# Edge bias from ScalarE to TensorE, and gather indices read straight from kept tables, in a four-layer graph network

## What is computed

```
loop = arange(N); src = concat(src, loop); dst = concat(dst, loop)
deg = segment_sum(1, dst);  dinv = rsqrt(deg)
xw = h @ W0
agg = segment_sum(xw[src] * (dinv[src] * dinv[dst]), dst) + b0
x = x + where(agg >= 0, agg, a0 * agg)
```

## Time and profile before

| | before |
|---|---|
| median of 3 runs | 2609.81 us (2604.56 to 2611.62) |
| profiled execution | 2608.14 us, span 2606.6 us |
| mean granted TensorE clock | 0.912 |
| PE busy | 1899.9 us (73%) |
| DVE busy | 2027.9 us (78%) |
| ACT busy | 1725.7 us (66%) |
| POOL busy | 1311.4 us (50%) |
| DMA | 446.18 MB, mean 171 GB/s |

### The profile page before, as it was taken

The page is one execution under the profiler, slowest core; times in us unless marked ns, Lnnn a source line. Parts: engine busy times, 40 slices in busy tenths (PEclk is TensorE's granted clock), DMA queues, the critical chain, the costliest instruction groups (busy, mean ns, idle before and its releaser), DMA issues. The chain is left out here.

```text
span 2606.6 us, 48448 instructions
## 1 busy us (share of the span) xinstructions
PE 1899.9 (73%) x9715; PEld 1275.5 (49%) x9715; DVE 2027.9 (78%) x8016; ACT 1725.7 (66%) x4230; POOL 1311.4 (50%) x1309
## 2 busy tenths in 40 slices
PE   2445668888855666578884899566663999999996
PEld 1134445555534555468883444233332555555553
DVE  6855579999968999688885888588885777777773
ACT  3655679999965777589991444699994444444441
POOL 6755656666637666277760000000002677777773
PEclk9878889999986888889996999799997999999998
DMA  7989986666645777556662443699996544445540
GB/s 134 220 147 183 153 203 193 198 195 195 194 130 159 222 223 224 176 165 198 201 181 72 128 129 86 185 305 308 305 308 215 128 100 107 106 113 114 115 106 21
DMA packets 376244, 446.18 MB, mean 171 GB/s; under 512 B 103667, under 2 KB 225338, under 8 KB 376082
## 3 DMA queue, kind: packets, MB, share of 16 engines
q1 hardware_dynamic: 309970, 368.09, 50.8%
q0 software_dynamic: 59840, 74.08, 12.3%
q10 hardware_dynamic: 6272, 2.06, 0.5%
HBM read 288.86 MB, written 185.03 MB: 182 GB/s over the span
## 5 line engine op out<-in xcount | busy, mean ns | idle before, releaser
L2380 POOL DMA_INDIRECT mlp_bx<-t_X,k_bslot x2 | 2.0, 1012 | 611.7 <-POOLq L2647 611.4
L526 POOL DMA_INDIRECT second_xs<-t_XX,second_irs x200 | 205.4, 1027 | 115.8 <-issue 49.3
L2398 POOL DMA_INDIRECT out_dram<-mlp_ou,mlp_iro x200 | 212.6, 1063 | 83.2 <-issue 71.3
L2391 POOL DMA_INDIRECT mlp_xs<-t_X,mlp_irs x200 | 213.8, 1069 | 80.7 <-issue 55.7
L526 POOL DMA_INDIRECT project_xs<-t_XX,project_irs x200 | 199.6, 998 | 62.9 <-issue 58.3
L526 POOL DMA_INDIRECT a_xd<-in_x_dram,a_ird x152 | 152.6, 1004 | 129.1 <-DVE first_xo L968 84.9
L2439 DVE TENSOR_TENSOR_SCAN mlp_ms<-mlp_fm,mlp_ms,mlp_mm 128x500 f32<-128x500 f32 x98 | 123.4, 1260 | 120.2 <-ACT mlp_mm L2515 112.9
L2515 ACT ACTIVATE mlp_mm<-mlp_ps_m,mlp_bn 128x500 f32<-128x500 f32 x100 | 67.7, 677 | 187.1 <-PE mlp_ps_m L2575 187.1
L2265 PE MATMUL x_ps_o<-x_ht,x_wd 128*128 128x512 f32 (+1 forms) x198 | 117.1, 675 | 97.2 <-DVE x_ht L2165 81.1
L2575 PE MATMUL mlp_ps_m<-mlp_e,mlp_wn 128*128 128x504 f32 x400 | 185.3, 586 | 0.0
L2562 PE MATMUL mlp_ps_e<-mlp_h,mlp_we 128*128 128x504 f32 x400 | 179.5, 592 | 2.9 <-DVE mlp_h L2448 1.5
(11 more groups left out here) (411 smaller groups left out, 6343.3 us busy)
## 6 DMA issues: line engine op xcount, KB each, us to landing
first_x<-in_x_dram SPq DMA_DIRECT2D x97, 256.0 KB, 4.3
t_XX<-first_x SPq DMA_DIRECT2D x97, 256.0 KB, 2.7
project_x<-t_XX SPq DMA_DIRECT2D x97, 256.0 KB, 3.3
x_x<-t_XX SPq DMA_DIRECT2D x97, 256.0 KB, 4.3
t_X<-x_x SPq DMA_DIRECT2D x97, 256.0 KB, 3.7
out_dram<-x_ou SPq DMA_DIRECT2D x97, 256.0 KB, 4.7
t_XR<-in_x_dram SPq DMA_DIRECT2D x23, 1000.0 KB, 13.4
t_G<-second_g SPq DMA_DIRECT2D x50, 267.8 KB
```

What stands on the lines that cost most here:

```text
L526: pool.indirect_dma_start(dst[:, q, lo:hi], None, table, bass.IndirectOffsetOnAxis(ap=idx[:, q:q + 1], axis=0)).then_inc(s_rows, 16)
L2391: pool.indirect_dma_start(Xs[u][:, q, :], None, T["X3"], bass.IndirectOffsetOnAxis(ap=irs[u][:, q:q + 1], axis=0)).then_inc(s_rows[u], 16)
L2398: pool.indirect_dma_start(out, bass.IndirectOffsetOnAxis(ap=iro[s][:, q:q + 1], axis=0), OU[s][:, q, :], None, bounds_check=N - 1, oob_is_ ...
```

## The change

The edge bias: L1042 is left out. VectorE's blend L958 takes the product z straight from PSUM in place of the biased Re, so Re = Qe * (1 - a0) + z. TensorE first writes the bias into all four tiles of psE with one matmul (a row of ones, 1 x 126, against the row b01r, 1 x 512), and then, after the wait for VectorE, adds Re turned by four plain matmuls against the identity that accumulate, in place of four transposes. TensorE's later waits for psY are on e_p (VectorE has read it) in place of e_q (ScalarE has). b01r is loaded in prep by four small DMAs on SyncE's queue, ahead of b1c, and VectorE adds b1 to it.

The indices: the ring copies and their semaphores go, in the first, second, project and mlp phases. GpSimd gathers (and in mlp scatters) with columns of the kept tables, and its bodies are written out (`straight`) in place of looped (`steps`), as the columns must be constants.

```diff
@@ prep @@
+        for q in range(GT):
+            sp.dma_start(kp.b01r[:, q, :], a["L0_gnn_b"].partition_broadcast(1)).then_inc(s_w, 16)
-        dve.wait_ge(s_w, 16 * (8 + GT))
+        dve.wait_ge(s_w, 16 * (8 + 2 * GT))
+        dve.tensor_tensor(kp.b01r[:, :, :], kp.b01r[:, :, :], kp.b1[0:1, :, :], ALU.add)
-        pe.wait_ge(s_w, 16 * (8 + GT))
+        pe.wait_ge(s_w, 16 * (8 + 2 * GT))
@@ first, GpSimd @@
-            gate(kp, pool, e_idx, t + 1)
+            src, dst = kp.srci[:, t * GT:(t + 1) * GT], kp.dsti[:, t * GT:(t + 1) * GT]
...
-                gather_rows(pool, Xs[u], T["XR"], irs[u], s_rows[u], 0, XR)
+                gather_rows(pool, Xs[u], T["XR"], src, s_rows[u], 0, XR)
...
-        steps(pool, NGE, 10, 0, body)
+        straight(NGE, 0, body)
@@ first, VectorE @@
-        def indices(g, s):
-            if there(g, NGE) and not before(g, 4):
-                dve.wait_ge(s_rows[s], complete(g - 4, s) + gathered[s])
-                dve.tensor_copy(irs[s][:, :], kp.srci[:, bass.ds(g * GT, GT)])
-                dve.tensor_copy(ird[s][:, :], kp.dsti[:, bass.ds(g * GT, GT)]).then_inc(e_idx, 1)
...
-            indices(t + 3, (u + 3) % 4)
...
-                dve.scalar_tensor_tensor(Re[:, :, :], Qe[:, :, :], kp.oma[:, 0:1], Re[:, :, :], ALU.mult, ALU.add).then_inc(e_p, 1)
+                z = psY[:, 0:W4].rearrange("p (q e) -> p q e", q=GT)
+                dve.scalar_tensor_tensor(Re[:, :, :], Qe[:, :, :], kp.oma[:, 0:1], z, ALU.mult, ALU.add).then_inc(e_p, 1)
@@ first, ScalarE @@
-                act.activation(Re[:, :, :], z, ACT.Identity, bias=kp.b01[:, 0:1])
@@ first, TensorE @@
                 if h == 1 and not before(t, 1):
-                    pe.wait_ge(e_q, t)
+                    pe.wait_ge(e_p, t)
...
             if there(g2, NGE):
-                pe.wait_ge(e_p, g2 + 1)
                 if not before(g2, 1):
                     pe.wait_ge(e_x1, g2)
+                pe.matmul(psE[0:RW, :], kp.ones[0:1, 0:RW], kp.b01r[:, :, :].rearrange("p q d -> p (q d)"),
+                          start=True, stop=False, skip_group_check=True)
+                pe.wait_ge(e_p, g2 + 1)
                 for q in range(GT):
-                    ins = pe.transpose(psE[0:RW, q * 128:(q + 1) * 128], Re[:, q, :], kp.ident[:, :])
+                    ins = pe.matmul(psE[0:RW, q * 128:(q + 1) * 128], Re[:, q, :], kp.ident[:, :],
+                                    start=False, stop=True, skip_group_check=True)
                 ins.then_inc(e_b, 1)
...
                 if not before(g1, 1):
-                    pe.wait_ge(e_q, g1)
+                    pe.wait_ge(e_p, g1)
@@ second; project alike with kp.idx2 @@
-                gate(kp, pool, s_idx, t + 1)
...
-                gather_rows(pool, Xs[u], T["XX"][0:ROWS, :], irs[u], s_rows[u])
-
-        steps(pool, NGE, 1, 0, body)
+                gather_rows(pool, Xs[u], T["XX"][0:ROWS, :], kp.idx[:, t * GT:(t + 1) * GT], s_rows[u])
+
+        straight(NGE, 0, body)
@@ mlp @@
-                gate(kp, pool, s_idx, t + 1)
...
-                                            bass.IndirectOffsetOnAxis(ap=irs[u][:, q:q + 1], axis=0)).then_inc(s_rows[u], 16)
+                                            bass.IndirectOffsetOnAxis(ap=kp.idx[:, t * GT + q:t * GT + q + 1], axis=0)).then_inc(s_rows[u], 16)
...
-                gate(kp, pool, s_io, g + 1)
...
-        steps(pool, NGE, 8, 0, body)
+        straight(NGE, 8, body)
...
-                dve.tensor_copy(iro[s][:, :], kp.sidx[:, bass.ds(g * GT, GT)]).then_inc(s_io, 1)
```

More of the change, by code:

```diff
@@ L212, in __init__ @@
         self.b01 = sb("b01", [128, 1])
+        self.b01r = sb("b01r", [1, GT, 128])
         self.oma = sb("oma", [128, 1])
@@ L715, in phase_first @@
     nb = [sb(f"nb{i}", [128, 2 * XD]) for i in range(2)]
-    Xs, Xd, irs, ird = kp.Xs, kp.Xd, kp.irs, kp.ird
+    Xs, Xd = kp.Xs, kp.Xd
     Xo = [sb(f"xo{i}", [RW, GT, 128]) for i in range(2)]
@@ L841, in body @@
             if before(t, NR):
[L842 removed]
+                gather_rows(pool, Xs[u], T["R"], src, s_rows[u], D, XR)
                 if t >= 4:
[L844 removed]
+                    gather_rows(pool, Xs[u], a["x"], src, s_rows[u])
             else:
[L846 removed]
+                gather_rows(pool, Xs[u], T["XR"], src, s_rows[u], 0, XR)
             if u and not before(t, 4):
                 gate(kp, pool, e_x1, t - 3)
[L849 removed]
+                gather_rows(pool, Xd[u], a["x"], dst, s_rows[u])
             if known(t) and t == NR - 1:
@@ L1155, in phase_second @@
     Xp = [sb(f"xp{i}", [RW, GT, 128]) for i in range(4)]
-    irs = [sb(f"irs{i}", [RW, GT], I32) for i in range(4)]
     st = [sb(f"st{i}", [RW, 2 * GT, 6]) for i in range(2)]
@@ L1226, in body @@
             if there(t, NGE):
-                gate(kp, pool, s_idx, t + 1)
                 if not before(t, 4):
                     gate(kp, pool, s_h, t - 3)
-                gather_rows(pool, Xs[u], T["XX"][0:ROWS, :], irs[u], s_rows[u])
-        steps(pool, NGE, 1, 0, body)
+                gather_rows(pool, Xs[u], T["XX"][0:ROWS, :], kp.idx[:, t * GT:(t + 1) * GT], s_rows[u])
+        straight(NGE, 0, body)
     @block.vector
     def _(dve):
-        def indices(g, s):
-            if there(g, NGE):
-                if not before(g, 4):
-                    dve.wait_ge(s_rows[s], landed(g - 4, s, 4, GT) + gathered[s])
-                dve.tensor_copy(irs[s][:, :], kp.idx[:, bass.ds(g * GT, GT)]).then_inc(s_idx, 1)
-        for g in range(3):
-            indices(g, g)
         dve.tensor_scalar(kp.idx2[:, :], kp.idx[:, :], float(N), float(SLOTS), ALU.is_ge, ALU.mult).then_inc(s_far, 1)
@@ L1495, in body @@
             if there(t, NGE):
-                gate(kp, pool, e_idx, t + 1)
                 if not before(t, 4):
                     gate(kp, pool, e_h, t - 3)
-                gather_rows(pool, Xs[u], T["XX"], irs[u], s_rows[u])
-        steps(pool, NGE, 1, 0, body)
+                gather_rows(pool, Xs[u], T["XX"], kp.idx2[:, t * GT:(t + 1) * GT], s_rows[u])
+        straight(NGE, 0, body)
     @block.vector
     def _(dve):
-        def indices(g, s):
-            if there(g, NGE):
-                if not before(g, 4):
-                    dve.wait_ge(s_rows[s], landed(g - 4, s, 4, GT) + gathered[s])
-                dve.tensor_copy(irs[s][:, :], kp.idx2[:, bass.ds(g * GT, GT)]).then_inc(e_idx, 1)
-        for g in range(3):
-            indices(g, g)
         dve.wait_ge(s_bd, 32)
@@ L2291, in phase_mlp @@
     Xd = [sb(f"xd{i}", [RW, GT, 128]) for i in range(8)]
-    irs = [sb(f"irs{i}", [RW, GT], I32) for i in range(4)]
-    iro = [sb(f"iro{i}", [RW, GT], I32) for i in range(4)]
     st = [sb(f"st{i}", [RW, 2 * GT, 6]) for i in range(2)]
@@ L2326, in phase_mlp @@
         sem("msg"), sem("msg_relu"), sem("y"))
-    s_ms, s_nb, s_zs, s_v, s_o, s_sc, s_io = (sem("summed"), sem("row_bias"), sem("source_norm"), sem("biased"), sem("out"),
-        kp.s_scattered, sem("out_idx"))
+    s_ms, s_nb, s_zs, s_v, s_o, s_sc = (sem("summed"), sem("row_bias"), sem("source_norm"), sem("biased"), sem("out"),
+        kp.s_scattered)
     gathered, scattered = kp.counts(GT, GT)
@@ L2395, in body @@
                 gate(kp, pool, s_o, g + 1)
-                gate(kp, pool, s_io, g + 1)
                 for q in range(GT):
-                    pool.indirect_dma_start(out, bass.IndirectOffsetOnAxis(ap=iro[s][:, q:q + 1], axis=0), OU[s][:, q, :], None,
+                    pool.indirect_dma_start(out, bass.IndirectOffsetOnAxis(ap=kp.sidx[:, g * GT + q:g * GT + q + 1], axis=0), OU[s][:, q, :], None,
                                             bounds_check=N - 1, oob_is_err=False).then_inc(s_sc[s], 16)
-        steps(pool, NGE, 8, 0, body)
+        straight(NGE, 8, body)
         for s in range(4):
```

16 lines of the change are left out of this document (4 added, 12 removed).

## The result

| | before | after |
|---|---|---|
| median | 2610.32 us (4 runs on the same chip) | 2638.66 us (2635.95 to 2643.59, 4 runs) |
| ratio to before | 1 | 1.0113, 95% interval 1.0094 to 1.0131 |
| span of the profiled execution | 2606.6 us | 2634.5 us |
| mean granted TensorE clock | 0.912 | 0.919 |

The change makes the kernel 1.1% slower. The forecast was 2619 us, with a range up to 2632: the direction came out as argued, the size was too small, and the time lies above the range.

A forecast was written before the change was run, and what follows sets the result against it. The prediction took the carry loop between ScalarE and TensorE to bound the first phase: 2608.1 + 14.6 (first phase) - 3.5 (second phase) - 1 (last phase) + 1 (preparation) = 2619 us, range 2594 to 2632.

The forecast's parts named there:

- The loop that bounds the phase: First phase: ScalarE's carry and TensorE's products, first carry to fourth, take 5.49 us against ScalarE's 4.50; 0.43 longer an iteration.
- The four signs named ahead: First phase: iteration near 11.1 us, ScalarE waiting about 1 us before the fourth carry, ScalarE not full, eight edge matmul instructions.
- the bias matmul at 0.86 us: First phase, TensorE: the one-row, 512-column matmul costs as much as the wide product L1089, bounded from 0.43 to 0.96.
- The bound of 0.1 us "for switching": First phase, TensorE: 0.1 us more for switching into and out of the accumulation, stated as 0.55 longer an iteration.
- Preparation: Four more loads ahead of TensorE's semaphore and one VectorE addition: 1 us more, bounds 0 and 2.3.
- Second phase: VectorE charged as the bound: 50 index copies of 0.07 us go, 3.5 us less, bounds 0 and 7.
- Project: 50 index copies go beside a full ScalarE: no change in time.
- Start of the last phase: GpSimd's waits for index copies, 18.3 us in six, go: 1 us less, bounds 0 and 6.
- A: First phase: ScalarE's removed pass decides, TensorE's additions cost 0.33 us or less; iteration 10.18, time 2586 us; chance 0.18.
- B: First phase: additions cost about 0.89 us, bias matmul at half; phase unchanged, small gains elsewhere, about 2605 us; chance 0.13.
- D: First phase: a plain float32 matmul costs four transposes, so edge matmuls take 1.76 us; time 2648 us; chance 0.03.
- C: Project: straight GpSimd code issues gathers 0.1 us slower, 15 us more over 50 iterations, 2634 us; chance 0.04.

The follow-up runs named there:

- x4: The changed kernel without the bias matmul, so the edge rows lack that bias; ratio 0.9936 to the kernel before, 10.25 us an iteration.
- x5: The changed kernel with the bias matmul issued an iteration earlier, in TensorE's idle time behind the fourth sums; ratio 0.9953 to the kernel before, 10.25 us an iteration.
- x3: The changed kernel with the bias matmul contracting 128 equal rows in place of one; ratio 1.009 to the kernel before, 11.06 us an iteration.
- x1: The kernel before with only the index part of the change; ratio 0.999 to the kernel before, 10.70 us an iteration.
- x2: The kernel before with only the edge part, ring copies and GpSimd loops kept; ratio 1.0118 to the kernel before, 11.44 us an iteration.
- x7: The changed kernel with the one-row bias matmul issued twice in a row; ratio 1.0447 to the kernel before, 13.45 us an iteration on the mean.
- x8: The changed kernel with the four bias-row loads later and on their own semaphore; ratio 1.0129 to the kernel before, 11.44 us an iteration.
- x17: The kernel of x6 with its one bias-row load on its own semaphore; ratio 0.9939 to the kernel before, 10.22 us an iteration.
- x6: The changed kernel with a one-row bias matmul into psY ahead of the edge product, four edge transposes kept; ratio 0.995 to the kernel before, 10.23 us an iteration.
- x9 to x16: Eight runs with late gathers: the changed kernel, x17's, two 128-row bias matmuls, and one 64-row bias matmul, each twice; ratios 0.9959 to 1.011 to the kernel before.

## Where the prediction was right and where it failed

**The loop that bounds the phase: right.** The sum was made over the chain from the first carry to the fourth, not over busy time. ScalarE lost 0.56 us of work and the iteration became longer, because TensorE's additions on that chain cost more than they freed. The four signs named ahead all showed: an iteration above 11, a wait of ScalarE before the fourth carry released by the carry matmul (1.20 us for "about 1"), ScalarE no longer full, eight edge matmul instructions. x4 and x5 show it from the other side.

**The step that failed: the bias matmul at 0.86 us, with no effect on its neighbours.** No row had a matmul of one contracted row, and I took the duration from the nearest one by columns, L1089. It costs 1.05 us itself, its neighbours 0.09 ahead and some 0.1 behind, together 1.24 in place of 0.86. That is 0.38 an iteration, 12.9 us over 34. Without them the measured 2638.7 us would be 2625.8, inside the range. The first phase's regular part lost 25.6 - 14.6 = 11.0 us beyond the sum, less than 12.9, since the other terms were a little too high: x3, without the extra, is 11.06 - 10.69 = 0.37 above the kernel before, where the sum had 0.43. The bound of 0.1 us "for switching" was named, but for the accumulation, not for the rows, and was nearly four times too small. (With it the sum gives 0.53 an iteration, not the 0.55 that it states.) The bounds were taken from rows with 126 and 128 contracted rows, so they could not hold this. The rule of the Trainium skill that I weighed (TensorE: Matmul & The Clock Gate, section "Why this matters for your kernels": as long with 32 rows as with 128) was not tried with 32 rows, but 1.05 us with 1 and with 64 rows against 0.86 with 128 don't bear it out where the neighbours use 126 or 128.

**The terms outside.** The last iterations of the phase pass through the same chain: 3.1 us that the sum left out, since it ended at the 34th iteration. Preparation: 1 forecast, 2.9 measured up to the first phase's start; between chips it varies by more than that, and x1, x2, x4, x5, x7 and x8 make the loads' own part 1.6 to 3.0 us, about at the bound of 2.3. Second phase: -3.5 forecast, -2.7 in the first pair, but 281.0, 282.0 and 282.7 us in x1 (copies gone), x2 (copies kept) and x17 (copies gone). A saving of more than 1 us there is not shown, and x1's interval allows at most 6 us for the whole index part. The step was to charge VectorE as the bound at 270 of 295 us, with 25 us of slack left. Project: nothing forecast, 2.0 longer, but as long in x2, which keeps the copies. Start of the last phase: -1 forecast, nothing to see. The node part of the third layer (-3.2) is touched by no edit and I can't explain it; it took between 330.8 and 334.4 us in the kernels run, in no order that follows the edits.

**The rivals.** A is out for the change as made, since the additions cost 1.70 us (1.24 + 0.46) and not 0.33; its mechanism is what x4 to x6 and x17 show, with a period of 10.1 to 10.25 where it said 10.18. B (the bias matmul at half) and D (edge matmuls at four transposes: 0.98 measured, not 1.76) are out by the rows, C by x1 against x2.

**What stays open.** The 0.38 us are read from start times. Whether TensorE waits until its work has run out, or only until the weights are loaded, no run tells apart, and that the tiling mode is the reason is inferred. Why two one-row matmuls bring the clock down in 24 of 34 iterations and not in the other ten is not settled, nor why one does at three places in x6 and x17 and nowhere in x5; a matmul of 96 rows was not tried. Why the phases with gathers took longer in x9 to x16 is not known; the kernel before did so too.

## What to carry to other kernels

Before moving work to an engine that has idle time, find the loop that sets the period and ask in which gap the work will stand: the same matmul cost 1.19 us an iteration inside the carry chain and nothing 5 us later in the same iteration. Between matmuls that contract 126 or 128 partitions, a matmul over one or 64 is not priced by its columns alone: take its own time and the late start of it and of its successor, or spread the value over 128 equal rows. The rows have to be filled, though: loaded by DMA ahead of the weights' semaphore, as in x3, they made the first phase start some 7 to 9 us later. When no row of the trace has the shape that you add, bound its effect on both neighbours too, and let the range reach there.

## What the runs showed of the hardware that was not expected

A float32 matmul of 512 columns takes 0.86 us from start to start with 128 contracted rows, 1.05 with 64 and 1.05 with 1, when its neighbours use 126 or 128; with its neighbours' delays the extra is 0.38 us, paid once for one such matmul or for two in a row (12.30 - 11.91 us and 11.44 - 11.06 us). The weight loads of the smaller matmul and of its successor start together with their matmuls, not 0.11 and 0.43 us ahead; the load of a second one-row matmul behind the first is again 0.43 us ahead. And two one-row matmuls in a row, 1.91 us of TensorE at 1.00, were followed by the 1.2 GHz level in 24 of 34 iterations though TensorE is recorded as busy in all of the window where it showed, while two 128-row ones left the clock at 1.00 in all 34.
